# Four GRU graph layers in blocks of 500 columns: another setup order and another overlap of neighbouring blocks

## The reference

```
for l in range(NUM_LAYERS):                       # 4
    m = x @ weight[l]
    agg = segment_sum(m[src], dst, num_segments=n_nodes)
    x = gru_cell(agg, x, w_ih, w_hh, b_ih, b_hh)
return layernorm(x0 + (x + x0), axis=-1)

gru_cell(inp, h):
    r = sigmoid(i_r + h_r);  z = sigmoid(i_z + h_z)
    n = tanh(i_n + r * h_n)
    return (1.0 - z) * n + z * h
```

## Time and profile before

| | us |
|---|---|
| median of three runs | 2376.01 (2375.49 to 2378.25) |
| the profiled execution, its own time | 2376.61 |
| its span | 2374.9 |
| busy PE | 2242.2 (94%) |
| busy DVE | 2234.1 (94%) |
| busy ACT | 1907.7 (80%) |
| busy POOL | 1723.2 (73%) |

### The profile page before, as it was taken

One profiled execution on the slowest core, in us unless ns is written; L12 is line 12 of the kernel. 1 busy time (PEld: TensorE's weight loads), 2 busy tenths in 40 slices (PEclk: granted clock), 3 DMA queues, 4 the chain that ended last, 5 costly groups with the idle time before them and its releaser, 6 DMA issues.

```text
span 2374.9 us, 49598 instructions
## 1 busy us (share of the span) xinstructions
PE 2242.2 (94%) x11836; PEld 1886.3 (79%) x11836; DVE 2234.1 (94%) x4557; ACT 1907.7 (80%) x3616; POOL 1723.2 (73%) x1645
## 2 busy tenths in 40 slices
PE   2799999999989999999979999999979999999996
PEld 1688888888768888888868888888868888888885
DVE  7799999999979999999969999999969999999998
ACT  1588888888768888888768888888857999999997
POOL 2677777777477777777567777777658888888884
PEclk7799999999999999999999999999989999999998
DMA  2355555555546555555546555555544555555554
GB/s 57 88 159 162 159 159 160 158 159 158 160 117 175 173 170 171 172 173 172 167 118 172 174 173 168 172 172 173 168 124 118 153 151 151 149 151 151 152 152 116
DMA packets 277065, 363.69 MB, mean 153 GB/s; under 512 B 107754, under 2 KB 186586, under 8 KB 276980
## 3 DMA queue, kind: packets, MB, share of 16 engines
q1 hardware_dynamic: 238196, 310.43, 43.8%
q0 software_dynamic: 38784, 52.30, 9.1%
HBM read 209.32 MB, written 179.81 MB: 164 GB/s over the span
## 4 chain that ended last, share of the span: by engine, by line
DVE 49%; issue 29%; ACT 10%; PE 9%; DVEq 2%; DMA 1%; POOL 0%; ACTq 0%; SPq 0%; POOLq 0%
DVE narg L1281 9%; DVE a_lo L1239 9%; DVE diff L1291 5%; DVE diff L1285 5%; DVE h_lo L1232 5%; ACT pA L954 3%; ACT pIN L954 3%; DVE aggT L1248 3%; PE pR L739 3%; DVE sel L1216 3%; DVE narg L1274 2%; DVE newT L1300 2%; PE pZ L739 2%; PE pA L727 2%; DVE bn L1316 2%
## 5 line engine op out<-in xcount | busy, mean ns | idle before, releaser
L591 POOL DMA_INDIRECT gath<-state,idx x900 | 945.9, 1051 | 259.2 <-issue 240.6
L571 POOL TENSOR_TENSOR h_lo<-hT,h_hi 128x252 fp32r<-128x252 f32 (+1 forms) x400 | 350.6, 876 | 246.3 <-ACT h_hi L916 159.6
L591 POOL DMA_INDIRECT gath<-in_x_dram,idx x300 | 343.7, 1146 | 108.7 <-issue 74.6
L950 ACT ACTIVATE rg<-pR,bsum 128x504 f32<-128x504 f32 x400 | 272.8, 682 | 100.9 <-PE pR L739 89.0
L1274 DVE SCALAR_TENSOR_TENSOR narg<-pHN,bhh,rg 128x504 f32<-128x504 f32 x400 | 294.7, 737 | 33.7 <-ACT rg L950 31.8
L727 PE MATMUL pA<-sel,g_lo 128*128 128x168 f32 x1188 | 285.5, 274 | 0.0
L727 PE MATMUL pA<-sel,g_hi 128*128 128x168 f32 x1188 | 273.2, 264 | 9.4 <-DVE g_lo L1227 4.8
L928 ACT CAST sel<-sel 128x504 fp32r (+1 forms) x400 | 246.4, 617 | 34.1 <-DVE flag_i L1223 33.9
L1291 DVE TENSOR_TENSOR diff<-zg,diff 128x504 f32<-128x504 f32 x400 | 272.7, 682 | 0.6
L958 ACT ACTIVATE zg<-pZ,bsum 128x504 f32<-128x504 f32 x400 | 270.2, 676 | 0.0
L727 PEld LDWEIGHTS pA<-sel,g_hi 128*128 128x128 f32 x1188 | 226.4, 191 | 30.4 <-issue 9.1
(11 more groups left out here) (212 smaller groups left out, 6500.3 us busy)
## 6 DMA issues: line engine op xcount, KB each, us to landing
columns<-newT SPq DMA_DIRECT2D x300, 252.0 KB, 2.1
hT<-columns SPq DMA_DIRECT2D x300, 252.0 KB, 2.7
state<-o_rows SPq DMA_DIRECT2D x300, 224.0 KB
x_rows<-in_x_dram SPq DMA_DIRECT2D x200, 224.0 KB
out_dram<-o_rows SPq DMA_DIRECT2D x91, 224.0 KB
gath<-state,idx POOLq DMA_INDIRECT x900, 2.5
state<-o_rows SPq DMA_DIRECT2D x300, 26.0 KB
idx<-edge_src SPq DMA_DIRECT2D x395, 1.5 KB
```

The costliest lines, as they stand in the source:

```text
L571: nc.gpsimd.tensor_tensor(h_lo[:, u % RING, cols], hT[:, u % RING, cols], h_hi[:, u % RING, cols].bitcast(F32), ALU.subtract).then_inc(s_h ...
L591: pool.indirect_dma_start(out=gath[:, u % RING, j, :], out_offset=None, in_=states[l], in_offset=bass.IndirectOffsetOnAxis(ap=idx[:, u % R ...
L950: nc.scalar.activation(rg[:, :], pR[:, 0:COLS], ACT.Sigmoid, bias=bsum[:, 0:1]).then_inc(s_r, 1)
```

## The change

**Columns.** `CP` is 125, a tile has 500 columns, and each state tile starts 502 columns after the one before (`HPITCH`). The edge sums in PSUM and the selections keep 4 x 126 columns (`SP`, `spaced`); what reads or writes them goes by rows of 125 (`by_rows`). In the last layer `spread` lets the identity passes read four overlapping pieces of 126 columns that start 125 apart, and the first block's passes are of the full width for each of three tiles.

```
-CP = ROWS + 1
+CP = ROWS
 COLS = RPP * CP
+SP = ROWS + 1
+HPITCH = COLS + 2
...
-SELW = COLS
+SELW = RPP * SP
...
-ROUNDS = P // 8
+ROUNDS = 15
+SLOTS = 8 * ROUNDS
...
-RAMP = 4
+RAMP = 3
+AHEAD = 4
...
+        def spread(parts, u):
+
+            whole = parts[:, :]
+            return bass.AP(whole.tensor, u % RING * HPITCH, [whole.ap[0], [ROWS, RPP], [1, SP]])
...
-                passes += [(sums_of, ident_r[:, :], part[:, u % RING, :], begins) for part, begins in ((h_hi, True), (h_lo, False))]
+                passes += [(spaced(pA), ident_r[:, :], spread(part, u), begins) for part, begins in ((h_hi, True), (h_lo, False))]
```

```
+            for l, whole in enumerate((rg, zg, narg, diff)):
+                pool.wait_ge(s_full, l + 1)
+                nc.gpsimd.tensor_tensor(wf_lo[:, l, :], whole[:, 0:3 * D], wf_hi[:, l, :].bitcast(F32),
+                                        ALU.subtract).then_inc(s_wlo, 1)
...
                 if isinstance(b, int) and b < RING and l == 0:
-                    pool.wait_ge(s_v, V_TABLES)
+                    pool.wait_ge(s_v, V_IDX)
```

```
-                        products_on_state(l, b, u, start, l < L - 1 and (l > 0 or exists_before(i, u, PRE)))
+                        r_on_state(l, b, u, start, l < L - 1 and (l > 0 or exists_before(i, u, PRE)))
+                        if not start:
+                            hn_on_state(l, b, u, start)
                         if first:
                             sum_first(l, start)
+                        if first and l:
                             z_on_state(l, 0, 0, start)
                         r_on_sums(l, b, u)
-                        if ramp and u == 3:
-                            sum_edges(l, 4, 4, False)
+                        if start:
+                            hn_on_state(l, b, u, start)
                         n_on_sums(l, b, u, l * NB + b - 1 if l or exists_before(i, u, 2) else None)
```

```
+                        if not ramp and exists(i, u, 1):
+                            summed()
+                            if final:
+                                divided()
                         r_times_hn(l, b, u)
...
+                        if opening and u >= RAMP - 1:
+                            gathered(2)
...
                         n_argument(l, b, u)
...
+                        elif exists(i, u, 1) and not (final and (not ramp or u == RAMP - 1)):
+                            divided()
...
-                        if l == 0 and exists(i, u, RAMP) and not ramp:
+                        if l == 0 and exists(i, u, AHEAD):
...
-                        if not ramp and exists(i, u, 3):
-                            low_gathered(l, *after(i, u, 3)[:2])
...
-                        if summed:
-                            low_part(l, *summed, final)
...
                         product(l, b, u)
```

329 lines of the change are left out of this document (182 added, 147 removed).

## The result

The changed kernel took 2436.67 us (median of four, 2434.75 to 2437.94), beside 2376.59 for the kernel before in the same session: a ratio of 1.0254, interval 1.0238 to 1.0270. The forecast was 2422, at most 2431. The direction was right, the size was not.

A forecast was written before the change was run, and what follows sets the result against it. No single bound: a ring of waits through VectorE and ScalarE in the first three layers, GpSimd in the last. 2376.6 -7.0 +0.9 +46.0 +0.3 +2 x (5.2-2.0+0.3) -1.0 = 2422.8, less 0.6: 2422 us; range 2368 to 2431.

The forecast's parts named there:

- 500 columns: Every block: 500 columns instead of 504 shorten VectorE and ScalarE instructions, -0.02 to -0.03 us a block.
- Steady step of layers two and three: Layers two and three: ScalarE's queue behind a_hi delays tanh by 0.08; 5.31 against 5.25 us, +5.2 us per layer.
- Steady step of the first layer, the term that decides: First layer: a_lo runs into GpSimd's h_lo, so the step is 6.19 us, +0.53 a block, +46 over 87 steps.
- The meeting: VectorE's a_lo starts inside GpSimd's h_lo and ends 0.55 us after it; bounds +0.10 to +0.6 a block, first layer.
- I am wrong in the main if a_lo in the first layer keeps its 0.68: Sign against the forecast: a_lo in the first layer stays at 0.68 us, where about 1.2 was forecast.
- The opening of a layer: First ten steps of a layer: net -2 us in layers two and three, +0.9 in the first.
- The setup: Before the first gather's sums: work leaves VectorE's chain for GpSimd and ScalarE, -7.0 us, bounds -8 and -4.
- The last layer: Last layer: GpSimd bounds it and its list is untouched but for 4 columns of a subtraction, -1 us.
- The first (2382: no meeting): First layer: a_lo and h_lo don't contend, or a_lo is first and keeps its place; step 5.76, total 2382; chance 0.16.
- the second (2357: the ring does not close): First three layers: ScalarE converts earlier, tanh stops waiting, the step falls to TensorE's need; total 2357; chance 0.14.
- the ring: Chain of waits closing a step; in the new order a_hi waits for agg, with tanh queued behind; +0.08 us remainder.
- The third: Rival: the last layer's overlapping passes run at half speed, or the selects are stretched too; total 2437; chance 0.08.

The follow-up runs named there:

- old overlap on new columns: Changed kernel's 500 columns and setup, with the step orders of the kernel before on TensorE, ScalarE and VectorE: 2424.46 us, ratio 0.9945.
- The mixed kernel: Changed kernel with `wf_lo` held back, h_hi before a_hi, z in PSUM and, in layers two and three, the step order of before; fourth session: 2346.36 us, ratio 0.9875.
- the z-in-PSUM run: Changed kernel with gate z left in PSUM instead of SBUF, TensorE's next z waiting for the product: 2442.62 us, ratio 1.0038.

## Why the prediction was right and wrong, by its steps

In short, the miss is not in the term that was said to decide. That one was put too high by 10.5 us, and the setup, the openings and the last layer too low by more, so part of the nearness of 2422 to 2437 is luck.

**500 columns.** Right: the commonest step of the old overlap on new columns is 5.22, and so is the fourth session's, against 5.25; that bears out 0.03 a block. It was mis-sized in one place: the whole h_lo of GpSimd fell by 0.088 us, not by the 0.01 a block in the -1 of the last layer.

**Steady step of layers two and three.** Right in mechanism and nearly in size: 5.35 for 5.31, with every instruction within 0.02 of its forecast place. The two steady parts grew by 7.3 and 6.8 us where 0.06 a block gives 4.8 each, 4.4 us of the miss.

**Steady step of the first layer, the term that decides.** The meeting is real: without GpSimd's reads the step is 5.79, as worked out. Its size was too great, +0.40 and not +0.53. The step that failed is "a_lo would end at 3.08+0.55=3.63, the selects start at 3.55 and take 0.67": it was built on two rows in which VectorE lost. In 67 of 80 blocks a_lo won, GpSimd's h_lo was stretched in its place, and the selections, which the prediction had as a mere bound, were held up instead. By its own last sentence, "I am wrong in the main if a_lo in the first layer keeps its 0.68", the prediction is wrong in the main here, and that the selections paid nearly the same price was luck. The prediction had weighed the page's rule (the Trainium skill, SBUF — State Buffer, "Who interferes with whom": whoever issues first holds the shared ports, the other waits) against the row of 89.64 and sided with the row. The runs say that neither gives the size: a_lo wins although its recorded start is 0.06 after GpSimd's, and the row of 89.64 lost with a start 0.39 ahead. (The prediction calls a spared a_lo its second rival; in its list it is the first.) Only the sum is steady, since the VectorE instruction that was held up ends 0.54 after GpSimd's h_lo whichever of them waits; and the page does name `tensor_scalar` among the instructions that can take both pairs, which fits the selections of 1.20. Over the 80 blocks this term was 10.5 us too dear (31.9 measured for 42.4), and it hid more than a third of the other misses.

**The opening of a layer.** Wrong, outside its own bounds: -2 forecast, +3.0 and +2.1 measured. The first two steps did gain 2.0 and 1.9 us together. But the last five of the ten blocks take 5.82 to 5.94 instead of 5.26, and the prediction, which had written "up to +0.45 a block for seven blocks", still netted to -2; and in the second layer the third block waits for a landing and then runs at the lower clock (9.07 for 5.84), a term that the prediction put at nothing. In the third layer that block takes 6.86, and 6.38, 6.40 and 6.15 follow. The mixed kernel, in which the old order has all these steps back near their old lengths, shows that they go with the new order. In the first layer the seven blocks take 6.58 on average (6.4 forecast), the opening +3.4 instead of +0.9.

**The setup.** Right in what leaves VectorE's chain, wrong in "GpSimd and ScalarE take them over and both have nothing else then". What mattered was not whether GpSimd was free but what VectorE did meanwhile: its range instructions took 6.49 us for 1.04. With `wf_lo` held back the start moved by -6.7, and by -6.6 in the mixed kernel, whose session is like that of the rows: nearly the forecast's -7.0.

**The last layer.** Wrong: "GpSimd's list is untouched" priced the instructions and not how long they last. The gathers of the bound engine wait for VectorE instructions with both operands in SBUF, and the new order puts two of these, g_lo and the product, in a row over the second gather; before, a_lo stood between them, which reads PSUM in this layer. The gathers took 14.8 us more against 7.1 gained on h_lo, and the step went from 5.96 to 6.06, where -1 was forecast: 7.7 us of the miss. Not all of the 14.8 is the new order's: with the old order on the new columns the gathers took 261.0 already, which used up what h_lo gained. The row was there to be seen: the earlier trace rows has 1058 ns as the mean of an instruction whose unhindered length is 1.00, and in the first layer the third gather averages 1.43.

**The rivals.** The first (2382: no meeting) and the second (2357: the ring does not close) are false. The third has the right time, 2437, for the wrong reason: the passes cost nothing, the selections are stretched but already inside the forecast's sum. Measured less forecast, the account is +5.4 (setup), -9.2 (first layer), +7.3 and +5.6 (second and third), +7.7 (last), -2.1 (behind the end), together the 14.7 between the forecast and the span.

**Left open.** Why the first three sessions have longer openings and, in the old order, a first layer of 5.96 a step; what the one step in ten of 6.3 to 6.5 waits for when h_hi stands first; what holds the old order's last layer at 474.5 when its gathers are short; and what decides which engine waits when two start within 0.06 us.

## What to carry to other kernels

Before work is given to GpSimd or moved on VectorE, put the two engines' time lines side by side and mark each VectorE instruction with two SBUF operands: under it GpSimd's subtractions and gathers must be counted as waiting, and the other way round; a filling with zeros did not wait. Where GpSimd was the bound, a product's operand left in PSUM was worth the whole stretch of the gather (23 us here for a changed operand and one wait), and in the old order, where another wait took over, 2.5 us. And where a loss has two causes, each remedy tried alone may show nothing. An order that suits one layer need not suit another: with z in PSUM in both, the new order is worth 13 us in the last layer (461.5 against 474.5), and it costs 2 to 3 us in the opening of each layer before it.

## What the hardware showed that was not expected

- A gather's issue on GpSimd is stretched by VectorE. In the last layer, all engines' time line of the changed kernel:

```profile
2014.79 2.13 POOL L636 DMA_INDIRECT gath<-state,idx  x1 [0.30 <-issue]
...
2015.28 0.67 DVE L1355 TENSOR_TENSOR diff<-zg,diff 128x500 f32<-128x500 f32 x1
2015.87 0.18 DVE L1397 SCALAR_TENSOR_TENSOR veps<-mv 125x20 f32<-125x20 f32 x1
```

  It ends at 2016.92, 0.87 after the end of the small instruction of 0.18 us at 2016.05. All 365 stretched gathers of the changed kernel end so, 0.86 to 0.91 us after such an end. The Trainium skill (SBUF — State Buffer, "Who interferes with whom") infers that `tensor_tensor` leaves the making of a DMA's descriptors on GpSimd alone. These rows and the z-in-PSUM run show that it does hold up an indirect gather. They don't show at which point: such a gather also takes its table `idx` from SBUF, and its wait may be for that read.
- VectorE's `TENSOR_SCALAR` with a single tensor operand in SBUF is held up by GpSimd's subtractions as well: three of 100x336 took 6.49 us for 1.04, three of 128x168 took 1.20 for 0.75.
- GpSimd's subtraction over 500 columns takes 1.194 to 1.198 us on average, over 504 it took 1.286. The single ones over 500 vary from 1.07 to 1.29 us in the last layer of the changed kernel, those over 504 from 1.27 to 1.30 in the kernel before.
- The same kernel takes 2375 us in some sessions and 2434 to 2437 in others. By the one trace of the kernel before from the second kind, almost all of the difference is in the first ten steps of each layer (35 us) and in the first layer's steady part (24 us).
